# Edge filters of an image tokenizer: from banded products over shifted columns to strip products read back from DRAM

## What is computed

```
gray = einsum('bchw,c->bhw', x, (0.2989, 0.587, 0.114))
edges = conv(gray, scharr, stride 1, padding 'SAME')    # two filters
h = sum over filters of |edges| / 2
h = concatenate([h, txt], axis=1)                       # (8, 384, 256)
h = h + attention0(layernorm(h))                        # 16 heads, two key sets
h = h + fp4_feed_forward(layernorm(h))
h = h + anchor_attention(layernorm(h))
h = h + expert_feed_forward(layernorm(h))               # shared and 8 experts
```

## Time and profile before

| | us |
|---|---|
| median of 3 runs (1815.18 to 1818.09) | 1815.2 |
| the profiled execution's own time | 1817.46 |
| its span, first to last instruction | 1815.7 |

### The profile page before, as it was taken

The page is one execution under the profiler, slowest core; times in us unless marked ns, Lnnn a source line. Parts: engine busy times, 40 slices in busy tenths (PEclk is TensorE's granted clock), DMA queues, the critical chain, the costliest instruction groups (busy, mean ns, idle before and its releaser), DMA issues.

```text
span 1815.7 us, 29086 instructions
## 1 busy us (share of the span) xinstructions
PE 1747.6 (96%) x9935; PEld 1115.4 (61%) x9935; DVE 1005.1 (55%) x2073; ACT 677.3 (37%) x1290; POOL 409.7 (23%) x415
## 2 busy tenths in 40 slices
PE   7989999899999998999999999999999999999997
PEld 3324444344444435777755666666767679999997
DVE  6597877778788898888865444443211112222221
ACT  2106656566666686545532322233010111111110
POOL 2101120110201003898722221110211211000000
PEclk9988999999999999999999999999999999999999
DMA  6832632426324402000074000000000003423211
GB/s 190 138 66 41 119 78 43 82 45 114 74 47 87 82 2 74 1 0 0 1 294 110 0 0 0 1 1 1 34 28 20 32 20 111 175 104 107 102 32 34
DMA packets 111955, 112.84 MB, mean 62 GB/s; under 512 B 11455, under 2 KB 104433, under 8 KB 111858
## 3 DMA queue, kind: packets, MB, share of 16 engines
q1 hardware_dynamic: 98610, 83.21, 20.3%
q10 hardware_dynamic: 9600, 18.92, 2.9%
q0 software_dynamic: 3648, 9.46, 1.4%
HBM read 78.51 MB, written 32.93 MB: 61 GB/s over the span
## 4 chain that ended last, share of the span: by engine, by line
PE 88%; DVE 7%; issue 2%; ACT 2%; DMA 0%; DVEq 0%; POOL 0%; ACTq 0%; POOLq 0%
PE ps_e L2218 11%; PE ps_e L2151 9%; PE ps_a L614 8%; PE ps_a L588 7%; PE ps_m L1651 6%; PE ps_a L603 6%; PE ps_e L2227 5%; PE ps_m L1794 5%; PE ps_e L2160 5%; PE ps_m L1722 4%; PE ps_m L1752 4%; PE ps_a L559 4%; PE ps_m L1667 3%; DVE mx L961 3%; PE ps_a L688 2%
## 5 line engine op out<-in xcount | busy, mean ns | idle before, releaser
L961 DVE TENSOR_REDUCE mx<-ps_a 128x1 f32<-128x384 f32 x768 | 379.7, 550 | 52.2 <-PE ps_a L588 50.4
L820 ACT ACTIVATE prob<-ps_a 128x768 f32<-128x768 f32 (+1 forms) x512 | 305.7, 650 | 96.7 <-PE ps_a L603 95.7
L588 PE MATMUL ps_a<-w,qs 96*128 96x384 bf16 x768 | 242.1, 338 | 7.7 <-DVE mx L961 3.8
L603 PE MATMUL ps_a<-qs,w 100*128 100x384 bf16 x768 | 207.1, 331 | 5.5 <-issue 4.0
L2218 PEld LDWEIGHTS ps_e<-xTr,w 128*128 128x128 f32 x1792 | 206.0, 193 | 2.2 <-issue 0.8
L2218 PE MATMUL ps_e<-xTr,w 128*128 128x128 f32 x1792 | 206.3, 276 | 0.6 <-DVE xTr L2394 0.6
L588 PEld LDWEIGHTS ps_a<-w,qs 96*128 96x128 bf16 x768 | 72.9, 98 | 182.2 <-DVE mx L961 103.6
L614 PE MATMUL ps_a<-prob,vp 128*32 128x384 f32 x1536 | 163.3, 498 | 0.0
L2151 PE MATMUL ps_e<-xT_all,w 128*128 x448 | 145.7, 486 | 0.0
L2283 ACT ACTIVATE gel_r<-ps_e 128x512 f32<-128x512 f32 x56 | 33.4, 597 | 280.9 <-PE ps_e L2218 280.9
L1651 PE MATMUL ps_m<-w 128*128 128x352 f32 x384 | 122.3, 462 | 2.2 <-ACT w L1828 1.2
(11 more groups left out here) (266 smaller groups left out, 2585.1 us busy)
## 6 DMA issues: line engine op xcount, KB each, us to landing
w<-parts_dram SPq DMA_DIRECT2D x192, 96.0 KB, 5.2
w<-in_L_ffn_W_dram ACTq DMA_DIRECT2D x18, 1024.0 KB, 8.3
parts_dram<-w SPq DMA_DIRECT2D x24, 576.0 KB, 3.4
qs<-parts_dram SPq DMA_DIRECT2D x96, 96.0 KB, 4.0
prob<-in_x_dram SPq DMA_DIRECT2D x24, 256.0 KB, 3.6
w<-in_L_ffn_W_dram SPq DMA_DIRECT2D x6, 1024.0 KB, 12.8
grouped_x<-empty_row SPq DMA_DIRECT2D x1, 4352.0 KB, 24.3
grouped_h<-empty_row SPq DMA_DIRECT2D x1, 4240.5 KB, 33.9
```

The costliest lines, as they stand in the source:

```text
L588: mm = pe.matmul(ps[:, r % 3, 0:T], qs[0:NS, b, u // 2, t * P:(t + 1) * P], ks[0:NS, b, u % 2, u // 2], start=True, stop=True)
L603: mm = pe.matmul(ps[:, scores_at(v, more) + t, 0:T], ks[0:NS + 4, b, kp, hh, t * P:(t + 1) * P], qs[0:NS + 4, b, hh], start=True, stop=True)
L820: act.activation(prob[:, g % 2, j, ts.start:ts.stop], ps[:, at + ts.start:at + ts.stop, 0:T], ACT.Exp).then_inc(exp_done.sem, 1)
L961: dve.tensor_reduce(at, ps[:, r % 3, 0:T], AX.X, ALU.max).then_inc(ring_free.sem, 1)
```

## The change

Gray values now go through DRAM. For each image the padded gray rows (258 columns) are stored into `gray_dram`, and three copies, one per column tap, bring back 34 rows for each of eight strips of 32 image rows: partition kx * 34 + j holds row j of every strip, shifted by kx. The nine taps of a filter then lie in one 102 x 32 matrix, and the filter of a strip is one product of 102 rows, 32 output rows and 256 columns; four strips stand side by side on PE. The `corner` product and ACT's `sides` copies are gone. The taps are loaded by three copies of 34 rows.

The order changes too. PE: weights, filters of image 0, projections of image 0, filters of images 1 and 2, then the maxima; the filters of images 3 to 7 stand in rounds 6, 16, 20, 24 and 28 of the maxima. Gray values of images 4 to 7 are scaled by ACT and added by POOL; POOL adds the two filters for images 2 to 7. ACT takes one square root at its very start.

```diff
+    gray_dram = nc.dram_tensor("gray_dram", [B, IMG + 2, IMG + 2], F32, kind="Internal").ap()
-    TAPS = [(f, kx) for f in range(2) for kx in range(4)]
-    BESIDE = 6
+    STRIP = 32
+    HALO = STRIP + 2
+    ROWS = 3 * HALO
+    STRIPS = IMG // STRIP
+    PAD = IMG + 2
+    BY_DVE = 4
+    CONV_AT = {6: 3, 16: 4, 20: 5, 24: 6, 28: 7}
...
             def image(i):
-                if i >= 2:
+                if 2 <= i < 2 + BY_DVE:
                     sp.wait_ge(gray_step.sem, gray_step.at(i - 1, 0))
+                elif i >= 2:
+                    sp.wait_ge(summed.sem, summed.at(i - 1 - BY_DVE, 0))
...
+            def store_gray(i):
+                if i < BY_DVE:
+                    sp.wait_ge(gray_step.sem, gray_step.at(i + 1, 0))
+                else:
+                    sp.wait_ge(summed.sem, summed.at(i + 1 - BY_DVE, 0))
+                sp.dma_start(gray_dram[i, 1:IMG + 1].rearrange("(a p) n -> p a n", p=P), grays[:, i]
+                             ).then_inc(gray_out[i % 2].sem, 16)
+
+            def strips(i):
+                sp.wait_ge(row_out.sem, 32)
+                sp.wait_ge(gray_out[i % 2].sem, gray_out[i % 2].at(i // 2 + 1, 0))
+                if i >= 2:
+                    sp.wait_ge(edges_done.sem, edges_done.at(i - 1, 0))
+                for kx in range(3):
+                    corner = gray_dram[i, 0:1, kx:kx + 1]
+                    rows = bass.AP(corner.tensor, corner.offset, [[PAD, HALO], [STRIP * PAD, STRIPS], [1, IMG]])
+                    sp.dma_start(im[kx * HALO:(kx + 1) * HALO, i % 2], rows).then_inc(im_in[i % 2].sem, 16)
+
+            for kx in range(3):
+                sp.dma_start(taps[kx * HALO:(kx + 1) * HALO].rearrange("p f a -> p (f a)"),
+                             scharr.rearrange("f o a b -> b (f o a)")[kx].partition_broadcast(HALO),
+                             allow_slow_non_contiguous=True).then_inc(taps_in.sem, 16)
             image(0)
+            sp.wait_ge(row_zero.sem, 1)
+            for row in (0, IMG + 1):
+                sp.dma_start(gray_dram[:, row], zero_row).then_inc(row_out.sem, 16)
...
+            store_gray(0)
+            strips(0)
             image(1)
...
+            image(2)
+            store_gray(1)
+            image(3)
+            strips(1)
+            store_gray(2)
...
             kinds(0)
+            strips(2)
+            store_gray(3)
             store_parts(0)
             stacks(0, 0, 0)
+            image(4)
+            strips(3)
+            image(5)
             stacks(0, 0, 1)
-
-            sp.wait_ge(edges_done.sem, edges_done.at(BESIDE, 0))
+            for i in range(4, B):
+                store_gray(i)
+                if i + 2 < B:
+                    image(i + 2)
+                strips(i)
+
             kinds(1)
...
+            def edge_rows(i):
+                pool.wait_ge(mag_done.sem, mag_done.at(i, 2))
+                pool.tensor_tensor(h[:, i * TT:i * TT + 2], mag[:, i % 2, 0], mag[:, i % 2, 1], ALU.add).then_inc(h_later.sem, 1)
+
+            def sum_gray(i):
+                j, g = i - BY_DVE, gray_of(i)
+                pool.wait_ge(scaled_done.sem, scaled_done.at(j, 2))
+                pool.wait_ge(borders.sem, 2)
+                pool.tensor_tensor(g, pix[:, i % 2, 0], pix[:, i % 2, 1], ALU.add).then_inc(summed.sem, 1)
+                pool.wait_ge(scaled_done.sem, scaled_done.at(j, 3))
+                pool.wait_ge(summed.sem, summed.at(j, 1))
+                pool.tensor_tensor(g, g, pix[:, i % 2, 2], ALU.add).then_inc(summed.sem, 1)
...
             for n in range(3 * KC):
                 low_parts(0, n)
+            edge_rows(2)
             for n in range(3 * KC):
                 low_parts(1, n)
+            sum_gray(4)
+            sum_gray(5)
+            edge_rows(3)
+            sum_gray(6)
+            edge_rows(4)
+            sum_gray(7)
+            for i in range(5, B):
+                edge_rows(i)
...
+            def edges(i):
+                u = i % 2
+                pe.wait_ge(im_in[u].sem, im_in[u].at(i // 2 + 1, 0))
+                if i >= 2:
+                    pe.wait_ge(mag_done.sem, mag_done.at(i - 1, 0))
                 else:
+                    pe.wait_ge(bands_done.sem, 6)
+                for f in range(2):
+                    for a in range(2):
+                        for c in range(STRIPS // 2):
+                            mm = pe.matmul(ps[c * STRIP:(c + 1) * STRIP, 4 + 2 * u + f, a * IMG:(a + 1) * IMG], band[0:ROWS, f],
+                                           im[0:ROWS, u, a * (STRIPS // 2) + c], start=True, stop=True, tile_position=(0, c * STRIP))
                     mm.then_inc(edges_done.sem, 1)
...
             for r in range(FIRST):
...
-                i, n = edge_piece(r)
-                if i is not None:
-                    edges(i, n)
+                if r in CONV_AT:
+                    edges(CONV_AT[r])
...
+            def scale_gray(i):
+                u = i % 2
+                act.wait_ge(pix_in[u].sem, pix_in[u].at(i // 2 + 1, 0))
+                for ch in range(3):
+                    act.mul(pix[:, u, ch], pix[:, u, ch], GRAY[ch]).then_inc(scaled_done.sem, 1)
...
-            act.wait_ge(borders.sem, 3)
-            sides(0)
-            sides(1)
-            magnitudes(0)
+            act.wait_ge(borders.sem, 1)
+            act.activation(rstd[:, 0:1], eps[:], ACT.Sqrt, bias=eps[:]).then_inc(root_done.sem, 1)
...
+            MOMENTS_AT = {2: 2, **{r + 3: i for r, i in CONV_AT.items()}}
             for r in range(FIRST + 1):
                 ring(0, first_ring(r))
...
+                if r in MOMENTS_AT:
+                    moments(MOMENTS_AT[r])
```

More of the change, by code:

```diff
@@ L261, in attention0 @@
         kind_rows = sb("kind_rows", [4, KINDS, T], BF16)
-        taps = sb("taps", [P, 2, 3, 3])
+        taps = sb("taps", [P, 2, 3])
+        band = sb("band", [P, 2, STRIP])
+        masks = sb("masks", [P, 3, STRIP])
         ps = ctx.enter_context(nc.psum_tensor("ps_a0", [P, 8, 512], F32))
@@ L704, in turn_weight @@
                 mm.then_inc(wTd.sem, 1)
-            pe.wait_ge(corner_in.sem, 32)
-            for n in range(len(TAPS)):
-                edges(0, n)
             pe.wait_ge(ident_done.sem, 1)
@@ L712, in _ @@
                 turn_weight(n)
-            for n in range(len(TAPS)):
-                edges(1, n)
+            edges(0)
             pe.wait_ge(wTe.sem, 5)
@@ L723, in _ @@
                 freed.append((signal, n + 1))
-            for i in range(2, BESIDE):
-                for n in range(len(TAPS)):
-                    edges(i, n)
+            edges(1)
+            edges(2)
             pe.wait_ge(rest_done.sem, rest_done.at(0, 3 * KC))
@@ L850, in roots @@
                 act.activation(rstd[:, tiles], mv[:, tiles, 1], ACT.Sqrt, bias=eps[:]).then_inc(root_done.sem, 1)
-            def sides(i):
-                gray, side = gray_of(i), side_of(i)
-                act.wait_ge(gray_step.sem, gray_step.at(i, 3))
-                act.wait_ge(side_zero.sem, 2 if i < 2 else 4)
-                for a, row in ((1, gray[0:1, 1, 0:IMG]), (0, gray[P - 1:P, 0, 0:IMG])):
-                    shifted = bass.AP(row.tensor, row.offset, [list(row.ap[0]), [1, 3], [1, IMG]])
-                    act.dma_start(side[3 * (1 - a):3 * (2 - a), 1 - a], shifted).then_inc(side_in[i].sem, 16)
-            act.wait_ge(borders.sem, 3)
-            sides(0)
-            sides(1)
-            magnitudes(0)
+            act.wait_ge(borders.sem, 1)
+            act.activation(rstd[:, 0:1], eps[:], ACT.Sqrt, bias=eps[:]).then_inc(root_done.sem, 1)
             for n in range(5):
@@ L868, in _ @@
                 act.copy(wT[:, n].rearrange("p k c -> p (k c)"), ps[:, n % 4]).then_inc(wTe.sem, 1)
+            magnitudes(0)
+            act.wait_ge(root_done.sem, 1)
             roots(0, 1)
-            sides(2)
-            magnitudes(1)
             for k in range(KC):
                 copy_inputs(0, k, k)
-            high_part(0, 0, KC)
-            roots(1, 2)
-            for n in range(1, 3 * KC):
+            for n in range(3 * KC):
                 high_part(0, n, (KC + n) % 4)
-                if n < 5:
-                    sides(n + 2)
             for n in range(2):
                 copy_v(0, 0, n, (4 * KC + n) % 4)
-            sides(7)
-            for i in range(2, BESIDE):
-                magnitudes(i)
-            for r in range(FIRST):
-                if r < len(PREPARE):
-                    step, n = PREPARE[r]
-                    if step == "inputs":
-                        copy_inputs(1, n)
-                    else:
-                        high_part(1, n)
-                i = edges_before(r, 0)
-                if i is not None:
-                    magnitudes(i)
-                if edges_before(r, 4) == B - 1:
-                    roots(2, B)
-            act.wait_ge(h_edge.sem, h_edge.at(B, 0))
+            magnitudes(1)
+            roots(1, 2)
+            magnitudes(2)
+            for step, n in PREPARE:
```

(24 more changed lines are left out.)

149 lines of the change are left out of this document (43 added, 106 removed).

## The result

The changed kernel takes **1939.6 us** (median of 4 runs, 1936.6 to 1942.5) against 1815.5 for the kernel before beside it: ratio 1.068, 95% interval 1.066 to 1.070. Forecast were 1932 and a range of 1890 to 1985. The profiled execution of it took 1942.5 us with a span of 1940.7, 125.0 us more than before. The attention loop's first scores start at 263.51 us instead of 138.20: 125.3 us later. So all of the loss lies ahead of the loop.

A forecast was written before the change was run, and what follows sets the result against it. It took PE's chain as the bound, with first scores at 138.2 us. Afterwards head 21.7, strips 153.4, gaps 59.6 and tail 19.8 sum to 254.5, 116.3 later; laid on median 1815.2: 1932 us, range 1890 to 1985.

The forecast's parts named there:

- Two engines: Strip copies: 34 rows dealt in equal shares run on two of 16 DMA engines, 19.2 us per image.
- issue of strips 0: Head before the loop: taps, pixels, gray and its store landing at 20.6 us, first strip 1.1 later.
- strips, issue to products, eight images: Strip loads: 408 pieces on each of two engines, 47 ns each, 19.2 us per image, 153.4 for eight.
- products to next issue, seven gaps: Queue between images' strips: stores, products and waits, 59.6 us counted from the end of strips to the next first strip.
- last products to first scores: Tail after the last strips: kind rows, parts store, stack issues, maxima copies and queued stack data; 19.8 us from landing.
- estimate of 59 ns: Strip reads starting off a 256-byte boundary fetch a fifth transaction on four: 59 ns per piece, some 39 us more.
- the gap ahead of image 3: Queue between strips 2 and 3: gray 3, image 0's parts, first half of the stacks, image 4's pixels; 18.6 us.
- The taps: Tap copies at the start: 306 tiny pieces per engine at 28 ns, 8.6 us; first band product near 10 us.
- The gain that gets lost: Ahead of the maxima: PE gives up 30.4 us of filters but waits for strips instead, so nothing shows.
- The first rival: Strips spread over all sixteen engines, 2.4 us per image; net 11 us faster, 1804; chance 0.08.
- the upper bound of the pace: Strip loads: 60 ns per 1 KB piece on each engine instead of 47, adding 42 us to the sum.
- the second rival: Each of an image's three strip copies on another engine pair: 6.4 us per image, start near 158, 1835; chance 0.06.

The follow-up runs named there:

- the wide copy: From the 36-row kernel: each image's three strip copies of 36 partitions became one copy of 108, so strips held other rows; 1818.6 us.
- the later statistics: From the 36-row kernel: DVE's statistics of image 3 stood three groups of maxima later; 1834.2 us.

## Why the prediction was right, point by point

**Two engines.** Right, and the step that carried all: the ends counted in the earlier trace rows and the shares in the earlier trace rows gave equal shares, 34 rows gave two engines, and the run series with 1, 2, 7 and 12 engines bears the arithmetic out, in its times and in its packet counts. The Trainium skill's rule (DMA: Bandwidth & Descriptors, "Why a DMA increments its semaphore by 16 and not by 1") agrees with all four.

**The sum by its terms.** From SP's issue of an image's strips to its products, and from the products to the next issue:

| term, us | predicted | measured |
|---|---|---|
| issue of strips 0 | 20.6 | 19.2 |
| strips, issue to products, eight images | 166.4 (8 x 20.8) | 182.2 (23.8, 21.8, 21.3, 29.2, 22.7, 21.0, 20.3, 22.1) |
| products to next issue, seven gaps | 48.4 | 43.4 (13.2, 0.8, 12.2, 14.8, 0.8, 0.8, 0.8) |
| last products to first scores | 19.3 | 18.6 |
| sum (before rounding 254.5 and 263.5) | 254.7 | 263.4 |

(The predicted 20.8 is 1.1 to the first packet, 19.2, and 0.5 for the landing; its gaps are shorter by 1.6 each here, for they were counted from landing to first packet.) The miss of 9 us is 16 in the strips, less 7 in the other terms. Not by their pace: 44.5 ns per 1 KB, near the lower bound of 44, is 18.2 us for 408 pieces instead of 19.2. The estimate of 59 ns for rows off a 256-byte boundary, worked out from the Trainium skill (DMA: Bandwidth & Descriptors, "How a descriptor splits into AXI transactions"), did not show; the measured 44.5 ns decides. What was too small is the rest of the wait. Images 5, 6 and 7, with no stacks beside them, took 2 to 4 us beyond their packets, not 1.6. And images 0 and 3 shared the two engines with others: image 0 with image 1's and 2's pixels (23.8), image 3 with the end of the first half of image 0's stacks and image 4's pixels ahead of its strips (the share was full until about 117 us), then with the second half of the stacks and image 5's pixels (29.2). I had put that traffic into the gap ahead of image 3 (17.0 taken, 12.2 measured), where part of it fell beside the strips instead and slowed them: the two misses partly cancel. That the sum came out within 9 us owes something to this luck.

**The taps.** Right in size (band product at 9.24, said near 10), wrong in mechanism: not 306 packets at 28 ns, since one, two, seven, twelve or sixteen engines bring them at 9.2 to 10.5 us. The term was a delay that the traces show and don't explain. It mattered little beside the strips.

**SP's hold.** Not foreseen: SP is held in the issue for 9 us per image. It seems to have cost little: the gray store behind it landed some 0.8 us after the strips' products had begun (78.85 after 78.09, 179.86 after 179.12, 201.62 after 200.88), so it waited for the same two engines in any case. No run took the hold away.

**The gain that gets lost.** As said: PE's 30.4 us of filters left the path and nothing of it showed.

**The first rival, 1804.** This is where the prediction was wrong, though its forecast did not rest on it. Even with twelve engines and spread partitions the change loses 9 to 11 us. Three steps of the rival failed. Strips on sixteen engines were to take 2.4 us: on twelve, where the same pace gives 3.4, they took 7.6 to land from SP's last issue, 5.6 when spread. The first maximum was to come at 57 us: with 36 rows it came at 73.3. Some 11 of these 16 us stood by image 0's normalised rows: its gray went out only at 13.8, its strips landed at 28.0, and the rows were ready at 36.2 instead of about 25 (28.4 in the kernel before). And the maxima were to give 8 us back: they gave 20, of which 5.5 were the wait for SP's copies, the rest with PE at half its clock for most of 100 to 150 us. That the clock is what made them slower is likely, and not shown. A change that had "worked as meant" would still have been a little slower; the 0.08 given to faster was too much rather than too little.

**Two slips in the working.** 7.8 us over 128 pieces are 61 ns, not 60, so the upper bound of the pace adds 46 us, not 42. And with 102 us less on the queue the second rival starts near 152 us and ends near 1829, not 158 and 1835. Neither touches the forecast; the first would put the top of the range some 3 us higher.

## What to carry to other kernels

Before a copy is cut into pieces for the engines, factor the number of its rows: 34 = 2 x 17 put 816 KB per image on two of sixteen engines, and two rows of padding (36) gave 107 us back. Count the engines from traces of other copies (the extra packet ends, the share when a copy is alone in flight) before believing in the bandwidth. And when part of a kernel is changed so that it yields other values, compare stages, not totals, if a later stage's work follows the data: 11 us of the wide copy's 14 were that. And when an edit shows nothing in the time, look whether its stage moved and another path ended last: the later statistics made the maxima 2.8 us faster, and PE waited 3 us longer for copies.

## What the runs showed of the hardware

- A copy's rows are dealt out in equal shares: 37, 34, 35 and 36 rows ran on 1, 2, 7 and 12 engines (q1's packets: 651, 0, 361 and 722 above those with 34 rows); one engine moved 23 GB/s, two 46, so 44.5 ns per 1 KB, at a source pitch of 1032 bytes.
- A queue whose copies sit on few engines holds the issuing engine: 9 to 13 us for three copies and 6 for a store behind them, against 1.25 us for three copies on twelve engines, and 2.42 when these go to every third partition.
- Where the twelve engines write matters: for image 0, 182 GB/s with strips (and the pixel loads beside them) that go into 36 neighbouring partitions, 251 to 261 with strips spread over 108. The stacks of the kernel before, at a full share and 142 GB/s, may be the same thing; that was not tried.
- At the lower clock sixteen products, four side by side on 32 columns each, took 3.64 us, and four of them, none side by side, 3.27.
- With PE busy for all of 24 us the granted clock stayed at 0.50 (1.2 GHz), having fallen at 96 to 104 us after PE had been busy for 9.16 of 12 us at full clock.
